# Fewer warm-up products and fewer fillers at the head of a fused attention and expert kernel

## The reference

```python
xn = layernorm_outer(x)                       # no gain, eps 1e-6
xf = layernorm(xn) * ln_g + ln_b
q, k, v = xf @ Wq, xf @ Wk, xf @ Wv           # 8 heads of 16 channels
attn = softmax(q k^T / 4) per row and head    # 128 x 128
t = x + (attn v * sigmoid(xf @ Wg + bg)) @ Wo + bo
tn = layernorm(t)
logits = mean over all tokens of tn @ Wr + br # one router decision for all tokens
two best experts e with shares s_e
y = sum_e s_e * (gelu(tn @ W1[e] + b1[e]) @ W2[e] + b2[e])
out = t + layernorm(y + tn) * gamma + beta
```

## Time and profile before

| | before |
|---|---|
| median of 3 runs | 96.31 us (95.89, 96.31, 97.31) |
| the profiled execution | 96.6 us |
| its span, first to last instruction | 94.5 us |
| granted TensorE clock, mean over the span | 0.941 |
| PE busy | 78.4 us (83%) |
| ACT busy | 63.9 us (68%) |
| DVE busy | 61.5 us (65%) |
| POOL busy | 61.4 us (65%) |

### The profile page before, as it was taken

The page is one execution under the profiler, slowest core; times in us unless marked ns, Lnnn a source line. Parts: engine busy times, 40 slices in busy tenths (PEclk is TensorE's granted clock), DMA queues, the critical chain, the costliest instruction groups (busy, mean ns, idle before and its releaser), DMA issues.

```text
span 94.5 us, 2850 instructions
## 1 busy us (share of the span) xinstructions
PE 78.4 (83%) x938; PEld 52.9 (56%) x938; DVE 61.5 (65%) x235; ACT 63.9 (68%) x153; POOL 61.4 (65%) x116
## 2 busy tenths in 40 slices
PE   1978767699899999999999989889978999999000
PEld 1725434366566674675665556558846748889000
DVE  0467386866798876978777879424746321776970
ACT  4247559669979999999999946672437646565410
POOL 5752969743986556755996746446469609989860
PEclk9999999999999999999999999999975579999955
DMA  1489354567329823555236950000000000000131
GB/s 40 158 209 341 109 101 75 111 119 113 74 37 73 160 57 64 111 111 111 58 71 130 88 111 10 0 3 0 7 0 0 0 0 0 0 0 0 56 111 56
DMA packets 18716, 6.79 MB, mean 72 GB/s; under 512 B 17232, under 2 KB 18128, under 8 KB 18704
## 3 DMA queue, kind: packets, MB, share of 16 engines
q1 hardware_dynamic: 18336, 6.21, 33.3%
q10 hardware_dynamic: 368, 0.43, 1.3%
HBM read 1.91 MB, written 0.52 MB: 26 GB/s over the span
## 4 chain that ended last, share of the span: by engine, by line
PE 37%; POOL 17%; DVE 15%; ACT 12%; issue 10%; DMA 5%; POOLq 1%; DVEq 0%; ACTq 0%
PE bank L999 6%; PE bank L944 5%; POOL rstd L705 5%; DVE stack L506 5%; DMA qk_t<-stack 5%; PE bank L1094 4%; ACT prob L349 4%; PE banks L999 4%; POOL stack L767 3%; PE banks L1004 2%; PE bank L954 2%; PE bank L918 2%; PE banks L1082 2%; ACT stack L326 2%; PE banks L903 2%
## 5 line engine op out<-in xcount | busy, mean ns | idle before, releaser
L506 DVE TENSOR_REDUCE stack<-banks 128x8 f16<-128x1024 f32 x16 | 19.3, 1208 | 0.3 <-PE banks L903 0.3
L349 ACT ACTIVATE prob<-banks 128x1024 f32<-128x1024 f32 x16 | 16.6, 1038 | 1.1 <-PE banks L930 1.1
L767 POOL TENSOR_TENSOR stack<-qkg,stack 128x256 f16<-128x256 f32 x16 | 11.1, 694 | 8.2 <-ACT qkg L328 8.0
L705 POOL TENSOR_TENSOR rstd<-rstd,neg_half 128x4 f32<-128x4 f32 (+1 forms) x13 | 13.0, 1002 | 1.1
L777 POOL TENSOR_TENSOR og<-og,rden 128x128 f32<-128x128 f32 x16 | 6.4, 402 | 9.1 <-DVE og L524 9.1
L514 DVE COPY q_t<-bank 128x512 f16<-128x512 f16 x16 | 6.8, 423 | 7.3 <-PE bank L918 7.3
L944 PE MATMUL bank<-prob,v_aug 128*32 128x128 f32 x256 | 10.3, 279 | 0.7 <-ACT prob L349 0.6
L326 ACT ACTIVATE stack<-bank 128x512 f16<-128x512 f32 x16 | 9.6, 600 | 0.9 <-PE bank L892 0.8
L357 ACT ACTIVATE u_sb<-bank 128x256 f32<-128x256 f32 x16 | 6.3, 393 | 5.3 <-PE bank L944 5.0
L328 ACT ACTIVATE qkg<-bank 128x384 f32<-128x384 f32 x16 | 8.0, 500 | 0.0
L954 PE MATMUL bank<-ident,u_sb 128*128 128x128 f32 x32 | 7.0, 301 | 0.8 <-ACT u_sb L357 0.6
(11 more groups left out here) (120 smaller groups left out, 183.0 us busy)
## 6 DMA issues: line engine op xcount, KB each, us to landing
w_in<-in_w SPq DMA_DIRECT2D x1, 512.0 KB, 5.4
out<-res SPq DMA_DIRECT2D x3, 128.0 KB, 1.8
x_all<-in_x SPq DMA_DIRECT2D x2, 128.0 KB, 2.8
x_all<-in_x SPq DMA_DIRECT2D x1, 256.0 KB, 3.1
w_in<-in_w SPq DMA_DIRECT2D x1, 256.0 KB, 5.6
b_b<-in_b SPq DMA_DIRECT2D x1, 256.0 KB, 5.7
qk_t<-stack SPq DMA_TRANSPOSE x16, 3.1
vectors_b<-in_vectors ACTq DMA_DIRECT2D x1, 160.0 KB, 3.4
```

The costliest lines, as they stand in the source:

```text
L349: nc.scalar.activation(prob[:, s % 2], s2_both_p, ACT.Exp, scale=HD ** -0.5).then_inc(exp_done, 1)
L506: nc.vector.tensor_reduce(q[:, :, :, SHIFT], s1_both_p, AX, ALU.max, negate=True).then_inc(max_done, 1)
L705: nc.gpsimd.tensor_tensor(rstd_[:, r], rstd_[:, r], neg_half[:, r], ALU.pow).then_inc(rstd_sem, 1)
L767: nc.gpsimd.tensor_tensor(stack_slots(b, 2, 0), qkg[:, b, 0:2 * INNER].rearrange("t (a h c) -> t a h c", a=2, h=HEADS), stack_slots(b, 0, ...
```

## The change

The warm-up loop is unrolled and made of ten products. Three of the same products stand behind the transposes of the first group of x. The fillers of the first steps become 2 in step 0, 4 before and 5 after the projection in step 1, and 6 (as before) in step 2. No semaphore, no transfer and no instruction of another engine is changed. The 15 products that go (6 warm-up, 9 fillers) and the 3 that come have the same shape and operands; the three new ones write bank 2, the bank of the warm-up products.

```diff
-WARM_START, WARM_NORM, WARM_ROUTING = 4, 1, 5
+WARM_START, WARM_NORM, WARM_ROUTING = 10, 1, 5
...
-            stay_warm(bank[B_S1][:, 0:256], ones[:, :].bitcast(F16), WARM_START)
+            for _ in range(WARM_START):
+                nc.tensor.matmul(bank[B_S1][:, 0:256], ident16[:, :], ones[:, :].bitcast(F16), start=True, stop=True)
             pe.wait_ge(fold_ok, 1)
             nc.tensor.matmul(w_p, fold[:, :, :].rearrange("d a c -> d (a c)"), w_in[:, 0:W_COLS], start=True,
                              stop=True).then_inc(w_folded, 1)
             transpose_x(0)
+            for _ in range(3):
+                nc.tensor.matmul(bank[B_S1][:, 0:256], ident16[:, :], ones[:, :].bitcast(F16), start=True, stop=True)
...
                 if t == 1:
-                    filler(8)
+                    filler(4)
                 if live(t):
                     project(t)
                 if t <= 2:
-                    filler(6)
+                    filler((2,5,6)[t])
```

## The result

The changed kernel takes 96.92 us in the median of 20 runs (96.12 to 98.82), the kernel before 96.30 us in the median of 20 (95.48 to 97.31). The ratio is 1.0062, with an interval of 1.0033 to 1.0092: 0.6 us slower, clear of noise and far inside 2%.

A forecast was written before the change was run, and what follows sets the result against it. The prediction took a chain of waits to bound the kernel, no engine being busy throughout. From the median of 96.31 us, +0.75 for a low-clock fold product and -0.45 for runs already paying it gave 96.6 us, range 95.6 to 97.9.

The forecast's parts named there:

- The ten products: Warm-up: ten products end at 4.07 us, so the fold product starts at 5.00 instead of 5.20, 0.20 us gained.
- The clock under the fold product: Fold product: runs at the low clock, 0.9 us longer (0.4 to 1.1); +0.75 us in all by row 0's `stack`.
- the pause: Ahead of the fold product: PE idle for 0.93 us after 2.1 us of work, so the clock stays low.
- The three new products: Behind the transposes: hidden ahead of the first projection at either clock, counted as nothing; at most 0.6 us if uncovered.
- The fillers: Steps 0 and 1: nine fewer, 1.0 us of PE time; row 1's projection 0.15 us earlier, counted as nothing.
- The halved term: Median of the kernel before: half of the 0.9 us is already paid there by some runs, so 0.45 us comes off.
- The unhalved sum: Whole kernel: 96.31 + 0.75 = 97.06 us, without taking off 0.45 us for slow fold products in runs of before.
- The second rival: Row maxima from 15.59 us on: less PE work leaves the clock low, +1.3 to 2.2 us, 97.9 to 98.8; chance 0.10.
- The third rival: Routing stage: its low-clock stretch moves against the work, at most 1.3 us gained, 95.0 to 95.6 us; chance 0.07.

The follow-up runs named there:

- fourteen_rest: The changed kernel with 14 straight warm-up products instead of ten; 98.18 us, ratio 1.0154 to the kernel before.
- ten_only: The kernel before with only the warm-up cut, from 16 looped to ten straight products; 99.09 us, ratio 1.0325.
- two_by_eight: The kernel before with its 16 warm-up products as two passes of eight instead of four of four; 98.56 us, ratio 1.0147.
- sixteen_rest_two: The changed kernel with 16 warm-up products executed, as eight passes of two; 97.29 us, ratio 0.9918 (0.9826 to 1.0011) to the kernel before.
- sixteen_rest: The changed kernel with 16 straight warm-up products instead of ten; 98.72 us, ratio 1.0271 to the kernel before.
- ten_same_code: The kernel before with ten warm-up products executed, looped so that four stand in the program as before; 97.53 us, ratio 1.0170.
- twelve_looped: The kernel before with its warm-up loop as three passes of four instead of four of four; 97.68 us, ratio 1.0083.

## Why the prediction held, and where it was off

The forecast was 96.6 us, slower by 0.3 within 2%; measured were 96.92, slower by 0.6. Step by step:

- **The ten products.** Right. The fold product starts 0.05 us behind `fold` and no longer behind the warm-up. In the one pair of traces it came 0.48 us earlier, of which 0.28 is x landing earlier and 0.20 the change.
- **The clock under the fold product.** Right in sign, in place and in size: 0.9 us were expected and 0.95 measured (2.07 against 1.12). The reason that it gave, the pause, is not shown: fourteen_rest had none and the same slow fold product. What the traces bear out is that ten to fourteen products were too few, five times of five. `w_hi` was expected at 7.05 and came at 6.83, the scaling at 8.29 and came at 8.07, both less by the 0.2 to 0.3 us that x was early; `stack` at 9.1 against 8.86 likewise. The step was worth more than the +0.75 us that went into the sum, since `stack` before began at 8.22 us and not at 8.32: 0.88 by the prediction's own 9.1, and 0.92 by the traces with x landing at the same time.
- **The three new products.** Right: hidden, by ten_only, though narrowly; `x_t` was ready at 7.71 us and the projection started at 7.76.
- **The fillers.** "I count nothing" was right at the high clock only. The prediction priced them there (row 1's projection 0.15 us earlier, worth nothing). At the low clock, which it forecast itself, the full ones hold ACT back, and thin ones save 0.75 us at row 1's `stack` and 0.24 at the second maximum of those two traces, which differ in the place of the code as well.
- **The halved term.** Too large by the traces. It took 0.45 us off because runs of before would pay for a slow fold product half the time. Of the nine traces with 16 or 18 products one has it low throughout and two in part. The unhalved sum, 97.06, stands nearer to 96.92, but with 0.92 in place of 0.75 it would be 97.23, and the halved one 96.78. The measured time lies between the two, so it doesn't decide how large the term should be. The Trainium skill ("TensorE: Matmul & The Clock Gate", section "What's actually happening") says that the moment of the rise varies from run to run; the traces agree (4.9 us before, beyond 14 us in two_by_eight with the same products). That half of the runs are late, as the prediction put it, they don't show.
- **The second rival, slower.** It had 0.10 and turned out to be a part of the result: in 3 of 20 runs the clock is low for longer, at 98.0 to 98.8 us, where it expected 97.9 to 98.8. Its price for one group was 0.64 us, and sixteen_rest_two's took 0.58 more. The place is shown in sixteen_rest_two's trace, at the row maxima of 14.8 us and after; the changed kernel's own three have no trace.
- **The third rival.** The low stretch in the routing stage does move and was worth nearly 1 us between the two traces, but it moves for both kernels.
- **What it didn't see.** That the count of products in the program matters by where PE's code loads fall. The changed kernel's trace shows no harm from it, and the change keeps the count.

Left open: no kernel gave back the 0.6 us in a ratio by restoring 16 or 18 products. sixteen_rest moved the code, and the four others with thin fillers scattered too much. The loss from fewer products is shown with full fillers only, at 0.8% to 1.7%; whether the pause or the smaller count delays the clock isn't. Why ten_same_code loses more than twelve_looped isn't settled either. Nor is it shown where the second of the 2 us goes by which a code load delays a transposing transfer.

## What to carry to other kernels

Warm-up products are worth what the first wide product behind them loses. Here too few of them cost more (0.95 us at the fold product) than too many (0.20 us of waiting behind them). Ending them just when the product can start was not enough: with fourteen that was so, and the fold product was still slow. Fillers have two sides, and both need the clock in the sum: at the low clock full ones hold the work back, and with thin ones the clock was low for longer in some of the executions, which the median and a single trace hide. Before a gain or a loss of 2 us is put down to an edit, check the landing times of the transfers and the loads on the instruction queue in both traces, and try the same executed instructions with another count in the program.

## What was unexpected in the hardware

A load on the instruction queue, one packet of 16 KB, that meets a transposing transfer goes with a landing up to 5.2 us behind its issue instead of 3.1, and in the one looked at closely (two_by_eight, 5.1 us) the last 12 of 1056 packets came only behind the load. Four products more in the program, with nothing else executed, made the kernel 1.5% slower (0.5% to 2.4%, from three runs). PE's work without a pause from 1.87 to 4.97 us left the clock low for what came next (fourteen_rest), where 16 or 18 products left it low throughout the fold product in one of nine traces. And the mean clock of a run separates kernels better than its time: 0.925 or less in 25 of 69 runs with thin fillers and the three new products against 2 of 121 with full ones.
